# The seam of mixer and cross attention: context laid out turned and split in the mixer's last output phase, first weights there too, last turns in four banks

## What is computed

```python
x = layernorm(x + masked_dense_gelu(x))
x = layernorm(x + autocorrelation(x, ctx, ctx))
x = layernorm(x + routed_lora(x))
x = layernorm(x + mixer(x))            # 128 heads x 64, 8 groups, gated, then y @ out_proj.T (8192 -> 512)
x = layernorm(x + cross_attention(x, ctx))
x = layernorm(x + mixed_lora(x))

def cross_attention(x, ctx):
    kv = concatenate([ctx, x], axis=1)           # 256 keys a batch
    q = rms_norm(x @ Wq)                         # 32 heads x 128
    k = rms_norm(kv @ Wk); v = kv @ Wv           # 8 key heads
    return softmax(q k^T / sqrt(128)) v @ Wo
```

## Time and profile before

| | |
|---|---|
| median of 3 runs | 2862.89 us (2861.46 to 2863.31) |
| the profiled execution's own time | 2862.68 us |
| its span in the profile | 2860.1 us |
| TensorE busy | 2585.0 us, 90% of the span |
| GpSimd busy | 1055.1 us, 37% |
| mean granted TensorE clock | 0.955 of full |
| mixer, output phase of the last group | 1738.7 to 1787.1 us |
| its last turns | to 1799.9 us |
| attention's preamble | to the first projection at 1823.5 us |

### The profile page before, as it was taken

How to read it: one execution, slowest core, us unless ns; L and a number is a source line. 1 busy time by engine, 2 the same in 40 slices (tenths; PEclk the granted TensorE clock), 3 DMA queues, 4 the chain that set the end, 5 groups by cost and what they waited for, 6 DMA issues and landing times. The chain is left out here.

```text
span 2860.1 us, 41040 instructions
## 1 busy us (share of the span) xinstructions
PE 2585.0 (90%) x14376; PEld 2112.7 (74%) x14376; DVE 1811.0 (63%) x2452; ACT 1083.2 (38%) x2201; POOL 1055.1 (37%) x838
## 2 busy tenths in 40 slices
PE   7777489999999999999999999689999999999958
PEld 4435377787777878778787887588888888878846
DVE  4564388696786967859678696264554644545553
ACT  2221233344333433334333343354454544544421
POOL 3000155564554655546555565222222122221210
PEclk9888799999999999999999999799999999999989
DMA  3000133031231312213123130200000000010010
GB/s 141 1 0 1 52 125 107 34 137 48 104 104 37 136 49 104 100 41 133 52 104 107 45 114 1 71 17 25 22 22 29 15 22 28 16 29 18 12 51 30
DMA packets 62092, 163.36 MB, mean 57 GB/s; under 512 B 8401, under 2 KB 9041, under 8 KB 53521
## 3 DMA queue, kind: packets, MB, share of 16 engines
q1 hardware_dynamic: 59808, 158.14, 16.1%
q10 hardware_dynamic: 2160, 3.43, 0.4%
HBM read 158.92 MB, written 2.62 MB: 56 GB/s over the span
## 5 line engine op out<-in xcount | busy, mean ns | idle before, releaser
L160 PE MATMUL pair<-XH,d_w_hi 128*128 128x512 f32 x1160 | 477.2, 411 | 54.0 <-DVE d_gated L1268 16.5
L162 PE MATMUL pair<-XH,d_w_lo 128*128 128x512 f32 x1160 | 463.1, 399 | 0.0
L161 PE MATMUL pair<-XL,d_w_hi 128*128 128x512 f32 x1160 | 460.5, 397 | 0.0
L1245 DVE TENSOR_TENSOR_SCAN d_decay<-d_decay,m_delta 128x1024 f32<-128x1024 f32 x128 | 366.3, 2867 | 42.4 <-DMA d_decay<-token_decays 42.4
L1152 POOL TENSOR_TENSOR d_decay<-d_decay,d_cb 128x1024 f32<-128x1024 f32 x128 | 309.7, 2420 | 135.1 <-DVE d_decay L1245 125.3
L1133 POOL TENSOR_TENSOR d_w_lo<-d_w,d_w_hi 128x512 fp32r<-128x512 f32 x144 | 193.9, 1347 | 308.1 <-ACT d_w_hi L1024 308.1
L160 PEld LDWEIGHTS pair<-XH,d_w_hi 128*128 128x128 f32 x1160 | 222.8, 192 | 110.3 <-issue 43.7
L162 PEld LDWEIGHTS pair<-XH,d_w_lo 128*128 128x128 f32 x1160 | 222.6, 192 | 51.8
L161 PEld LDWEIGHTS pair<-XL,d_w_hi 128*128 128x128 f32 x1160 | 223.2, 192 | 45.0
L1230 DVE SCALAR_TENSOR_TENSOR d_hs<-pair,d_conv,d_hs 128x1016 f32<-128x1016 f32 (+2 forms) x192 | 243.0, 1266 | 20.3 <-ACT d_hs L1049 15.8
L1157 POOL TENSOR_TENSOR d_gated_lo<-d_gated,d_gated_hi 128x512 fp32r<-128x512 f32 x128 | 165.6, 1297 | 199.5 <-ACT d_gated_hi L1068 199.5
(11 more groups left out here) (275 smaller groups left out, 6133.9 us busy)
## 6 DMA issues: line engine op xcount, KB each, us to landing
d_decay<-token_decays SPq DMA_DIRECT2D x64, 1024.0 KB, 4.8
d_w<-in_L_w_groups SPq DMA_DIRECT2D x144, 256.0 KB, 2.6
e_w<-in_L_w_heads SPq DMA_DIRECT2D x80, 256.0 KB, 2.6
d_wo<-in_L_wo_groups SPq DMA_DIRECT2D x64, 256.0 KB, 4.9
X<-in_x SPq DMA_DIRECT2D x8, 256.0 KB, 10.7
b_ctx<-in_ctx SPq DMA_DIRECT2D x8, 256.0 KB, 11.8
e_ctx<-in_ctx SPq DMA_DIRECT2D x8, 256.0 KB, 2.7
out<-X SPq DMA_DIRECT2D x8, 256.0 KB, 2.0
```

The source lines that it names most:

```text
L160: pe.matmul(out, wh, xh, start=first, stop=False)
L161: pe.matmul(out, wh, xl, start=False, stop=False)
L162: return pe.matmul(out, wl, xh, start=False, stop=last)
L1245: v.tensor_tensor_scan(r, r, m["DELTA"][:], 0.0, ALU.mult, ALU.add).then_inc(q["decay"], 1)
```

## The change

- The context comes in as a second input that is already turned by the host's layout (`ctx_t`, 512 x 1024), so nothing of it is turned on the chip. It is loaded as four pieces `e.CR[:, k]` of 512 KB, into space of the mixer's decay tile, after the mixer's last `scan`; ScalarE copies each piece to its high part in the last output phase (batches 1 to 4, 128x1024 each) and GpSimd subtracts (batches 2 to 5, 128x1024 each).
- The first four weight items of the attention are loaded behind them, copied on ScalarE (batches 3 to 6) and split on GpSimd (batches 4 to 7), in space of the mixer's weights and of its `d_cb`.
- The 33 counters of the attention are set by SP during the mixer's last group, and `begin_at_start` of the attention stage, with its meeting of the engines, is gone.
- The mixer's last turns go round four banks (0, 1, 6, 7): `turn(b)` waits for `turned_lo(b-4)`. On ScalarE and VectorE nothing of their order changes.
- In the attention stage the preamble and the first four loads, copies and splits are gone; TensorE waits for the context's four splits, and for the norm weights (`const`) only before the first `q_ssq`.

```diff
+class AttentionEarly:
+    def __init__(self, c, ctx_t, w_heads):
+        slab = c.nc.sbuf_base
+        c.keep("de_slab", [P, 2 * KD * T + 9 * D + T])
+        self.areas = {"decay": slab, "w": slab + 4 * 2 * KD * T, "cb": slab + 4 * (2 * KD * T + 9 * D)}
...
+        self.CR = self.place("e_ctx", [P, KD, T], F32, "decay", KD * T)
+        self.CH = self.place("e_ctx_hi", [P, KD, T], F32R, "decay")
+        self.CL = self.place("e_ctx_lo", [P, KD, T], F32R, "decay", KD * T)
...
-def turn(c, pe, s, b, bank):
+def turn(c, pe, s, b, bank, ring=1):
     pe.wait_ge(s.normed, b + 1)
-    if b:
-        pe.wait_ge(s.lo, b)
+    if b >= ring:
+        pe.wait_ge(s.lo, b - ring + 1)
...
+        def x_bank(b):
+            return c.bank[(0, 1, 6, 7)[b % 4]]
...
                 group(GM - 1, True)
+
+                for handle in e.q.values():
+                    sp.sem_inc(handle, START)
+                sp.sem_inc(e.begun, 1)
+                sp.wait_ge(q["y_ready"], START + GM * JT)
+                for k in range(KD):
+                    sp.dma_start(e.CR[:, k, :], e.ctx_t[k * P:(k + 1) * P, :]).then_inc(e.ctx_in[k], 16)
+                for i in range(EARLY):
+                    if i >= 2:
+                        sp.wait_ge(e.q["w_split"], START + i - 1)
+                    sp.dma_start(e.WR[:, i % 2, :], e.w_heads[0, i, :, :]).then_inc(e.w_in[i % 2], 16)
...
                         if last_group and b >= 3:
-                            turn(c, pe, s, b - 3, c.bank[0])
+                            turn(c, pe, s, b - 3, x_bank(b - 3), 4)
...
                         if last_group and b >= 4:
-                            turned_hi(c, act, s, b - 4, c.bank[0])
+                            turned_hi(c, act, s, b - 4, x_bank(b - 4))
+                        if last_group and b <= KD:
+                            act.wait_ge(e.ctx_in[b - 1], 16)
+                            act.activation(e.CH[:, b - 1, :], e.CR[:, b - 1, :], ACT.Copy)\
+                               .then_inc(e.ct["hi"], 1)
+                        if last_group and 3 <= b < 3 + EARLY:
+                            i = b - 3
...
+                            act.wait_ge(e.w_in[i % 2], 16 * (i // 2 + 1))
+                            act.activation(e.weight(e.WH, i), e.WR[:, i % 2, :], ACT.Copy).then_inc(e.q["w_hi"], 1)
...
                         if last_group and b >= 2:
                             norm_rstd(c, pool, s, b - 2)
+                        if last_group and 2 <= b < 2 + KD:
+                            k = b - 2
+                            pool.wait_ge(e.ct["hi"], k + 1)
+                            pool.tensor_tensor(e.CL[:, k, :], e.CR[:, k, :], e.CH[:, k, :].bitcast(F32),
+                                               ALU.subtract).then_inc(e.ct["lo"], 1)
+                        if last_group and 4 <= b < 4 + EARLY:
+                            i = b - 4
...
+                            pool.wait_ge(e.q["w_hi"], START + i + 1)
+                            pool.tensor_tensor(e.weight(e.WL, i), e.WR[:, i % 2, :],
+                                               e.weight(e.WH, i).bitcast(F32), ALU.subtract)\
+                                .then_inc(e.q["w_split"], 1)
...
-        c.begin_at_start(q)
...
-                for b in range(NB):
-                    if b >= 2:
-                        sp.wait_ge(ct["turned"], b - 1)
-                    sp.dma_start(CTX[:, b % 2, :], ctx_dram[b]).then_inc(ctx_in[b % 2], 16)
...
-                for b in range(NB):
-                    pe.wait_ge(ctx_in[b % 2], 16 * (b // 2 + 1))
...
-                pe.wait_ge(ct["lo"], NB)
...
-                pe.wait_ge(const, 17)
+                pe.wait_ge(ct["lo"], KD)
                 project_q(0, 0)
...
-                for i in range(4):
-                    w_hi(0, i)
...
-                for i in range(5):
-                    w_lo(0, i)
+                w_lo(0, EARLY)
```

More of the change, by code:

```diff
@@ L93, in end_stage, with place, weight @@
         self.sems = []
+class AttentionEarly:
[3 more added lines that the diff above has]
+        self.areas = {"decay": slab, "w": slab + 4 * 2 * KD * T, "cb": slab + 4 * (2 * KD * T + 9 * D)}
+        self.nc = c.nc
+        self.ctx_t, self.w_heads = ctx_t, w_heads
+        self.CR = self.place("e_ctx", [P, KD, T], F32, "decay", KD * T)
+        self.CH = self.place("e_ctx_hi", [P, KD, T], F32R, "decay")
+        self.CL = self.place("e_ctx_lo", [P, KD, T], F32R, "decay", KD * T)
+        self.WH = self.place("e_w_hi", [P, 4, KD, P], F32R, "w")
+        self.WL = self.place("e_w_lo", [P, 4, KD, P], F32R, "w", 4 * D)
+        self.WR = self.place("e_w", [P, 2, D], F32, "cb")
+        held, c.sems = c.sems, []
+        self.w_in = [c.sem(f"e_w_in{i}") for i in range(2)]
+        self.ctx_in = [c.sem(f"e_ctx_in{k}") for k in range(KD)]
+        self.begun = c.sem("e_begun")
+        self.ct = sems(c, "e_ctx_", "hi lo")
+        self.q = sems(c, "e_", "w_hi w_split kv_proj k_sq k_var k_rk k_norm k_turned k_hi k_lo v_hi v_lo q_proj q_sq "
+                               "q_hi q_lo q_ssq q_var rq scored max negmax exp rsum probs pt_ready pt_hi pt_lo o_ready "
+                               "o_hi o_lo out_ready acc")
+        self.sems, c.sems = c.sems, held
+    def place(self, name, shape, dt, area, words=0):
+        return self.nc.alloc_sbuf_tensor_at(name, shape, dt, offset=self.areas[area] + 4 * words)
+    def weight(self, ap, i):
+        return ap[:, {2: 0, 3: 1, 0: 2, 1: 3, 4: 2, 5: 3}[i], :, :].rearrange("p k n -> p (k n)")
+EARLY = 4
 class NormSems:
@@ L793, in _, with stage_mixer @@
                                   c.bank[2 + h][:, :]).then_inc(q["copied"], 1)
-def stage_mixer(c, m, w_groups, wo_groups, rows):
+def stage_mixer(c, m, w_groups, wo_groups, rows, e):
     nc = c.nc
@@ L1013, in _ @@
                 for b in range(NB - 3, NB):
-                    turn(c, pe, s, b, c.bank[0])
+                    turn(c, pe, s, b, x_bank(b), 4)
             @block.scalar
@@ L1123, in _ @@
                 for b in range(NB - 4, NB):
-                    turned_hi(c, act, s, b, c.bank[0])
+                    turned_hi(c, act, s, b, x_bank(b))
             @block.gpsimd
@@ L1288, in acc @@
                         if last_group and 4 <= b < NB:
-                            turned_lo(c, v, s, b - 4, c.bank[0])
+                            turned_lo(c, v, s, b - 4, x_bank(b - 4))
                         if b < NB:
@@ L1333, in _, with layer1_mixer @@
                 for b in range(NB - 4, NB):
-                    turned_lo(c, v, s, b, c.bank[0])
-def layer1_mixer(c, a):
+                    turned_lo(c, v, s, b, x_bank(b))
+def layer1_mixer(c, a, e):
     nc = c.nc
@@ L1348, in layer1_mixer, with stage_cross_attention @@
         c.end_stage()
-        stage_mixer(c, m, a["L1_w_groups"], a["L1_wo_groups"], rows)
+        stage_mixer(c, m, a["L1_w_groups"], a["L1_wo_groups"], rows, e)
         c.end_stage()
-def stage_cross_attention(c, ctx_dram, w_heads, norm_w):
+def stage_cross_attention(c, e, w_heads, norm_w):
     nc = c.nc
@@ L1384, in stage_cross_attention @@
         MX, NM, SUM, RS = (sb("e_" + n, [P, 2, GQ]) for n in "mx nm sum rs".split())
-        w_in = [c.sem(f"e_w_in{i}") for i in range(2)]
-        ctx_in = [c.sem(f"e_ctx_in{b}") for b in range(2)]
+        w_in, ct, q = e.w_in, e.ct, e.q
+        c.sems = c.sems + e.sems
         const = c.sem("e_const")
[L1388 to L1391, removed]
-        c.begin_at_start(q)
         s = NormSems(c, "e")
@@ L1413, in _, with turn_ @@
                 sp.dma_start(NW[:], norm_w).then_inc(const, 16)
-                for b in range(NB):
-                    if b >= 2:
-                        sp.wait_ge(ct["turned"], b - 1)
-                    sp.dma_start(CTX[:, b % 2, :], ctx_dram[b]).then_inc(ctx_in[b % 2], 16)
-                def turn_(kh):
-                    for i in range(NI):
+                def turn_(kh, items):
+                    for i in items:
                         sp.wait_ge(q["w_split"], START + kh * NI + i - 1)
@@ L1423, in turn_ @@
                                      .rearrange("o p n -> p (o n)")).then_inc(w_in[i % 2], 16)
-                with sp.Fori(0, HK) as kh:
-                    turn_(kh)
+                turn_(0, range(EARLY, NI))
+                with sp.Fori(1, HK) as kh:
+                    turn_(kh, range(NI))
             @block.tensor
             def _(pe):
-                for b in range(NB):
-                    pe.wait_ge(ctx_in[b % 2], 16 * (b // 2 + 1))
[L1431 to L1436, removed]
-                pe.wait_ge(ct["lo"], NB)
                 def project_q(kh, n):
@@ L1455, in q_ssq @@
                     pe.wait_ge(q["q_sq"], START + kh * NQ + n + 1)
+                    if n == 0 and isinstance(kh, int):
+                        pe.wait_ge(const, 17)
                     if n == 0:
@@ L1598, in _ @@
             def _(act):
[L1599 to L1602, removed]
                 act.wait_ge(const, 17)
```

25 lines of the change are left out of this document (15 added, 10 removed).

## The result

The changed kernel takes 2850.12 us (median of 5 runs, 2847.2 to 2856.0), against 2862.88 us before (5 runs beside it): a ratio of 0.9961, 95% interval 0.9946 to 0.9975. It is faster, by 11 us (7 to 15), and not by the 22.2 that were forecast; 2850.1 lies outside the range of 2835 to 2846. The profiled execution was the slowest of the five: 2856.0 us, span 2854.2.

What follows compares the result with a forecast made beforehand. TensorE, busy 90% of the span, was taken to bound the kernel, with its gaps. Gains of 27.9 us less 4.7 for GpSimd's subtractions and 1.0 for the port gave 22.2: 2862.68 to 2840.5 us, range 2835 to 2846.

Steps and rivals of the forecast that it cites:

- Part 1, the preamble: Between SP's start of the attention and the first projection: 19.96 us of preamble go, a gain of 19.9 us.
- Part 2, counters and meeting: At the border from mixer to attention: without counter settings and one meeting, 3.61 us shrink to 0.96, gain 2.6 us.
- Part 3, four banks: In the mixer's last turns: a bank for each lets turns follow their own norms, a gain of 5.4 us.
- the case named there: In the last turns: if the last turn has the full clock, the four banks gain 5.8 us, not 5.4.
- The gross sum: Gains from preamble, counters with one meeting, and four banks: 19.9 + 2.6 + 5.4 = 27.9 us.
- Part 4: In the last output phase: TensorE waits for GpSimd's added subtractions, mainly at batches 3, 5 and 6, a loss of 4.7 us.
- The port: In the last output phase: four norms on VectorE contend with GpSimd for shared ports, costing 1.0 us within bounds 0 and 2.2.
- the forecast's other case: In the last output phase: norms that waited run ahead of GpSimd's next instruction each time, a port cost of 2.2 us.
- or a later stage that moves: Last item in the list of what would prove the forecast wrong: a stage after the change altering its time; no size given.
- the rivals: Alternative outcomes: splits hidden 10%, splits dearer or border stays 20%, slower through the clock 2%, nothing gained 1%.
- Dearer splits: In the last output phase: large subtractions cost 4.3 us each, or the border stays; 2844 to 2849 us, chance 20%.

Runs made afterwards that it cites:

- e3: The kernel before with the four banks alone, for all eight turns of the mixer: 2858.3 us, 0.9979 of before.
- e1: The kernel after with the slab, and so the mixer's weight halves, moved by 32 bytes: 2852.82 us, 0.9959 of before.
- e4: e1 with the last output phase's helper work dealt out anew, VectorE doing three of four large subtractions: 2845.98 us, 0.9933 of before.
- e2: The kernel before with the mixer's weight halves moved by 32 bytes and the buffers behind by 64: 2873.39 us, 1.0029 of before.
- p2: The kernel before with only the buffers behind the mixer's weight halves moved, by 64 bytes: 13.98 us per head pair (before 14.00).
- q1: The kernel before with weight halves 448 bytes later and x's halves 384 bytes later: 13.89 us per head pair (before 14.00).
- q3: The kernel after with 160 unused bytes ahead of the slab, putting the weights at x's phase, and 352 behind: 2830.52 us, 0.9887 of before.
- q2: The kernel before with the weight halves moved to 83840 and 89984, 256 past x's phase within 512 bytes: 13.90 us per head pair (before 14.00).
- p1: The kernel before with both weight halves and all mixer buffers behind them 64 bytes later: 13.93 us per head pair (before 14.00).
- q4: e4 with all operands of mixer, attention and last stage at one phase within 512 bytes: 2830.62 us, 0.9889 of before.

## Why the prediction was wrong

- **Part 1, the preamble: right.** 19.96 us from SP to the first projection became 0.20: 19.8 against 19.9. The norm weights' load is covered, and the first projection begins at the low clock as before (steps of 0.43 us).
- **Part 2, counters and meeting: right.** 3.61 us became 1.01: 2.6 against 2.6.
- **Part 3, four banks: right.** From the last matmul to the last split 13.02 us became 7.41: 5.6 against 5.4, and e3 shows 5.5 for it alone. The last turn had the full clock, the case named there.
- **The gross sum** was to be 27.9. From the last matmul of the output phase to the first projection there were 36.59 us and there are 8.62: 28.0.
- **Part 4: right in place and nearly in size.** The idle times are 1.35, 1.56 and 1.14 us at batches 3, 5 and 6 (forecast 1.45, 1.7, 1.4), the large subtraction 2.40 us. The phase is 6.1 us longer, and the forecast with the port was 5.7, but part of that agreement is luck: some 1 us of the 6.1 is the longer stretch at the low clock with which the phase began, which the forecast didn't have. Free of that (e1 less e4) the new work costs 5.0. e4 shows that dealing the work out anew removes it.
- **The port: a size that isn't shown.** The forecast took 1.0 us for what reaches TensorE. VectorE did wait: the norms of 0.55 us took 1.37, 0.60, 0.67 and 1.66, 2.1 us over in all. That isn't the 2.2 of the forecast's other case, which was to be GpSimd's delay: GpSimd's large subtractions kept their 2.40 us, and only the pairs of `gated_lo` took 2.73, 2.73 and 2.70, about 0.2 over two single ones, 0.6 in all. The Trainium skill ("SBUF — State Buffer", section "Who interferes with whom") has the one that issues first hold the ports for its whole instruction and the other wait; the traces agree in that the slow norms end only after the GpSimd instruction beside them (45.81 after 45.53), but by the recorded starts the one that waits isn't the later one: the norm of the earlier trace rows starts 0.01 us ahead of the addition, and the norm of 1.66 us at 1795.47, 0.10 ahead of the `gated_lo` beside it. What of this reached TensorE lies within the 5.0.
- **The step that failed** is a term that the sum put at nothing without a reason. The sum names every added and removed instruction and takes all others to cost what they did ("or a later stage that moves" was the only guard, and it was an earlier one that moved). The change also moves the mixer's weights, and the mixer, none of whose projections it edits, became 14.8 us longer: 9.4 by the pace of its 48 pairs, 3.2 at its borders, 1.7 at its groups' starts. e2 with p2 shows that such a move alone suffices, q1 that the distance to x is what counts, and q3 that putting it right brings 20 us, more than was lost, since the kernel before wasn't in phase either.

The terms close on the profiled executions (from matmul to matmul): 0.7 ahead of the mixer, +14.8 in the mixer, +6.1 in the output phase, -28.0 at the seam, +0.5 behind: -5.9 us, the difference of the spans. The medians differ by 12.8; that the profiled run was the slowest of its five (5.9 us over its median) accounts for most of the rest. Without the 14.8 the sum would have been 20.7.

None of the rivals was this one. "Dearer splits" would have given 2844 to 2849, near the result for the wrong reason. The forecast also took the runs to lie within 0.06% of each other; 23 later runs of the kernel before lie between 2857.8 and 2870.1 us, 0.4%.

## What to carry to other kernels

A change that re-lays memory edits every instruction that reads it: before the sum, list the tiles whose address changes and the number of instructions on the bounding engine that read them, and price a few ns each (here 4.6 ns on each of 3456 matmuls). Read the period of an unedited steady loop in both traces first; a change of 1% there, constant over all repetitions, points to something other than scheduling. Where a matmul loop is bound by TensorE, a gap of some bytes that puts both operands at the same place within 256 is a cheap thing to try, and the period of the loop tells whether it helped.

## What the runs showed of the hardware

- The pace of back-to-back matmuls (128x128 weights, 512 columns, both operands fp32r) depends on the distance of the two operands in a partition, modulo 256: mean steps of 227.4 to 228.1 ns at 0 (five kernels), 229.1 to 229.4 at 192, 232.5 to 232.6 at 128, 233.2 at 224, 234.0 at 96. What in the memory does it wasn't found; in the mixer 32, 64 and 160 weren't tried.
- The runs of one kernel differ by up to 13 us, and the granted clock goes with it (of the kernel before, 2857.83 us at a mean of 0.957 and 2870.09 at 0.953). Two borders of groups in q3's trace, the same 20 us of the same work: in the first the clock stayed up, and the next pair of heads followed after 57.26 us, in the second it fell, and it was 59.38 us.

```profile
725.70:745.70 20.00, 18.41 (x110) 15.22 (x109) 13.53 (x11) 4.46 (x6) 6.46 (x8) 1.00 0.33 107
...
903.90:923.90 20.00, 17.92 (x83) 14.50 (x83) 11.56 (x10) 2.58 (x4) 6.23 (x7) 0.91 0.32 107
```

This fall cost 2.1 us. Of the six borders between groups the kernel after met it at four, q1, q2 and p1 at none. Over all profiles it came at 3 of 30 borders where both operands were in phase (q1, q2, p1, q3, q4) and at 27 of 54 in the nine other kernels. That doesn't mean that the clock falls less often in phase. It also falls at the groups' starts, between the `silu` of a group's last pair and that of the next group's first, and there the count is the other way round: in 32 of 35 such stretches in phase, in 32 of 63 in the others. Up to its last output phase the mixer was at 1.2 GHz for 62 us in the mean of the five kernels and for 61 in the mean of the nine. So the placement sets the pace; with it goes the place at which the clock falls, not how long it is low, and the cause of that is open.
